# A decoder kernel: self and cross attention taken in turn batch by batch, cross with one product per head, gates on 128 rows

## The chip, the cores and the metric

The kernel runs on one core of one Trainium2 chip. The metric is the device time of one execution in microseconds (us). A core has TensorE for matrix products (PE; its weight loads are listed apart as PEld), VectorE (DVE), ScalarE (ACT), GpSimd (POOL) and the SyncE queue (SP), which here only starts DMA transfers. Each engine takes its own instructions strictly in the order in which the program gives them; engines wait for each other by semaphores. Products land in PSUM, eight banks of 128 rows by 512 values.

## The reference

32 sequences ("batches") of 128 positions and 128 channels go through two decoder layers. In layer 0, self attention, cross attention and a mixture of gated experts each read a layer-normalised copy of x and add to x. Layer 1 (causal attention, a latent cross attention, experts with ReLU) comes after and isn't touched.

```python
# layer 0, per batch of x (128, 128); 16 heads of 8 channels
h = layernorm(x)
q, k = rope(h @ Wq + bq), rope(h @ Wk + bk);  v = h @ Wv + bv
x = x + softmax(q k^T / sqrt(8)) v @ Wo + bo               # self attention
h = layernorm(x)
q = h @ Wq' + bq';  k, v = ctx @ Wk' + bk', ctx @ Wv' + bv'  # ctx (128, 96)
s = clip(q k^T / sqrt(8), -1e4, 1e4)
x = x + softmax(s) v @ Wo' + bo'                            # cross attention
h = layernorm(x);  g = top2_gates(h @ router)               # 8 routed experts, 2 shared
x = x + sum_e g[e] * (silu(h @ w1[e]) * (h @ w3[e])) @ w2[e]
```

If anything in the cross scores is not a number, the reference replaces the attention by a constant; the kernel keeps a copy of x (x_before) for that case.

## The kernel before

One call of `attention` handles self and cross attention: 32 self batches, then 32 cross batches, in 16 groups of 4. Each engine runs a list of steps. `ORDERS` gives, for a kind of attention and an engine, the steps of one slot n in order; `steps` (L293) walks n, turns each entry into a batch or group and sorts what falls into the slot by **place in its list divided by the length of that list**. A plain name works on batch n plus a fixed lead (`AHEAD`): T, f0, f1, e0, e1, x0, x1 on n itself; m (on PE and on ACT), mc, q0, q1 on n+1; s0, s1, m0, m1, km2 on n+2; km on n+3; w and n on n-1; y and a on n-2. An entry such as `k^6` works on a whole group, once, in the slot 6 ahead of the group's first batch.

The steps, by engine:

- PE: `s0 s1` scores by query into the two S banks (L407 ff.), each waiting until DVE has reduced the pair before; `T` scores by key into four T banks, 12 products, waits for POOL's masked queries and for the exponentials of the batch before; `m` turns the row maxima round (L463); `f0 f1` subtract the maxima from T (L450); `w` multiplies probabilities by values (L465 ff.); `y` the output projection; group steps `x c` transpose inputs, `k k2 q q2 v` project them (L387 to L389). y, x, c and all projections share one bank, PB, and each waits until the one before has been read.
- ACT: `m` copies the negated maxima (L560); `e0 e1` exponentials of two T banks each (L553); `ln` layernorm (L588); `xh ch kh qh` round to a high part; `k q` evict cross projections.
- DVE: `m0 m1` row maxima (L626); `x0 x1` clip cross scores in place in T (L632); `a` adds the output to x; `n` normalises the heads; `q q2 k k2` rotate self projections; `mo` moments; `xl cl cs ks qs v` low parts, sums and values.
- POOL: `mc` clips cross maxima (L807), waiting for m1; `km km2` masked keys and `q0 q1` masked queries (L784), one tile of 128x512 each; `kt qt` finish the rotation; `kl ql` low parts (L780); `rs` four small steps that turn moments into deviations (L752 to L758); `bo` adds the bias to x.

Moments, deviations and normalised input have one buffer each for all groups: `mo` of a group waits for `rs` of the group before it, `rs` for that group's `ln`. Tiles of keys and queries have two places, used in turn by group number.

Self attention multiplies each head's probabilities once, by values with a column of ones (`ONE_PASS`, 16 products, 32 records in the trace for one batch), and `n` has four DVE steps: transpose, reciprocal, product, transpose. Cross attention multiplies twice, by the values and by `head_ones` (L484, 32 products, 64 records), and `n` has two steps: a reciprocal of 128x128 and a product.

In the experts, `transpose_gates` turns 16 columns of gates into 16 rows, ACT copies them, and `spread_gate` multiplies them by a selection of 16 rows.

## Time and profile before

| | us |
|---|---|
| runs shown (3) | 1337.65, 1343.76, 1350.34 |
| their median | 1343.76 |
| the profiled execution | 1335.86 |
| its span, first to last instruction | 1333.8 |

| engine | busy us | share of the span |
|---|---|---|
| PE | 1108.2 | 83% |
| PEld | 825.9 | 62% |
| DVE | 887.8 | 67% |
| ACT | 675.6 | 51% |
| POOL | 792.0 | 59% |

Loading and set-up fill the first 45 us or so, self attention runs to about 270, cross attention to 512, the gated experts to about 700, and layer 1 from there. Shares over the whole span mix stages with different limits, so the stages are read one by one. A matmul's end is modelled in the profile, so a busy PE is not a PE at its peak. PEclk is the granted TensorE clock as a share of 2.4 GHz. In a view by stretches, the number after a stretch is its length, and each engine's busy time has its instructions in brackets. A row of the timeline merges equal instructions that follow each other; the bracket at its end is the idle time of the engine before it and what ended that.

### The profile page before, as it was taken

The page shows a single profiled execution, that of the slowest core. Times are in us where ns is not written, and L with a number is a line of the kernel's source. Part 1 is how long each engine was busy: PE and PEld are TensorE (multiplying, and loading weights), DVE is VectorE, ACT ScalarE, POOL GpSimd, SP SyncE. Part 2 cuts the span into 40 slices and gives each one's busy share as a digit, 9 for nine tenths or more (in the row PEclk, how much of TensorE's full clock was granted, in tenths as well). Part 3 has the DMA queues.
Part 4 walks back from the last instruction along what each step waited for, and adds up shares of the span by engine and source line. Part 5 has one row for each costly group of instructions (what it writes and reads, how often), then busy time and mean ns, then how long its engine had stood idle before and what let it go on. Part 6 is the DMA issues. An engine that isn't in the chain of part 4 may idle for free. (4 is left out here: it accounts for less than half of the span.)

```text
span 1333.8 us, 30226 instructions
## 1 busy us (share of the span) xinstructions
PE 1108.2 (83%) x10619; PEld 825.9 (62%) x10619; DVE 887.8 (67%) x2152; ACT 675.6 (51%) x1304; POOL 792.0 (59%) x895
## 2 busy tenths in 40 slices
PE   1799997788888886899969999993799886599992
PEld 0566665555555556566636766662788885488881
DVE  3588887579999994766536777764799886322223
ACT  1355554435545442455425565645888653255551
POOL 4788875546555552444446766743888676754542
PEclk9999998679999997799979999995999887699996
DMA  9930000000000000000000000000000002376665
GB/s 345 381 112 2 2 2 7 9 15 16 16 22 15 10 10 1 0 1 1 1 0 2 2 2 2 2 2 19 13 13 8 13 26 78 114 216 199 195 188 192
DMA packets 51556, 75.20 MB, mean 56 GB/s; under 512 B 13118, under 2 KB 31683, under 8 KB 51152
## 3 DMA queue, kind: packets, MB, share of 16 engines
q1 hardware_dynamic: 43344, 60.57, 14.4%
q0 software_dynamic: 4544, 8.47, 1.9%
q10 hardware_dynamic: 3520, 4.23, 0.9%
q8 instruction: 87, 1.43, 0.4%
q14 instruction: 61, 0.50, 0.1%
HBM read 40.37 MB, written 31.70 MB: 54 GB/s over the span
## 5 line engine op out<-in xcount | busy, mean ns | idle before, releaser
L626 DVE TENSOR_REDUCE maxes<-bank 128x8 f32<-128x1024 f32 x192 | 233.6, 1217 | 52.1 <-PE bank L418 51.2
L553 ACT ACTIVATE self_probs<-bank 128x1024 f32<-128x1024 f32 x128 | 129.0, 1022 | 45.2 <-PE bank L450 44.7
L1521 POOL DMA_INDIRECT returned<-relu_y,relu_slots x78 | 76.3, 979 | 68.4 <-DVE relu_y L1497 55.0
L1458 ACT ACTIVATE relu_hidden<-bank,cols 128x256 f32<-128x256 f32 x156 | 73.8, 473 | 77.1 <-PE bank L1417 77.1
L784 POOL TENSOR_TENSOR self_k_hi_m<-self_kq_hi,const 128x512 fp32r<-128x512 f32 x64 | 66.5, 1039 | 74.8 <-ACT self_kq_hi L581 74.8
L560 ACT ACTIVATE self_neg_max<-bank 128x512 fp32r<-128x512 f32 x64 | 38.2, 596 | 133.2 <-PE bank L463 133.2
L1417 PE MATMUL bank<-latent_kq,relu_w_tile 128*128 128x256 f32 x312 | 94.8, 387 | 0.5 <-DVE latent_kq L1491 0.5
L1425 PE MATMUL bank<-relu_hidden,relu_w_tile 128*128 128x256 f32 x312 | 93.1, 381 | 0.0
L1491 DVE COPY latent_kq<-bank 128x256 f32<-128x256 f32 x39 | 16.6, 425 | 100.2 <-PE bank L1407 100.2
L632 DVE TENSOR_SCALAR bank<-bank 128x1024 f32<-128x1024 f32 x64 | 78.2, 1224 | 3.3 <-PE bank L438 3.3
L2402 POOL DMA_INDIRECT routed<-latent_rows,latent_place_i x64 | 62.6, 979 | 24.4 <-issue 22.2
L450 PE MATMUL bank<-self_neg_max,const_r 32*128 32x512 f32 x256 | 62.8, 481 | 9.2 <-DVE bank L632 5.7
L1310 POOL TENSOR_TENSOR ffn_hidden<-ffn_product,ffn_gate 128x512 f32<-128x512 f32 x32 | 41.0, 1280 | 44.0 <-ACT ffn_gate L1068 36.1
L553 ACT ACTIVATE causal_probs<-bank 128x1024 f32<-128x1024 f32 x64 | 64.4, 1021 | 4.9 <-PE bank L450 2.5
L784 POOL TENSOR_TENSOR self_q_hi_m<-self_kq_hi,const 128x512 fp32r<-128x512 f32 x64 | 66.6, 1040 | 0.2 <-PE bank L450 0.2
L784 POOL TENSOR_TENSOR self_q_lo_m<-self_kq_lo,const 128x512 fp32r<-128x512 f32 x64 | 66.5, 1039 | 0.2 <-issue 0.2
L784 POOL TENSOR_TENSOR causal_q_lo_m<-causal_kq_lo,const 128x512 fp32r<-128x512 f32 x32 | 33.5, 1046 | 55.1 <-PE bank L450 55.0
L463 PE MATMUL bank<-ident,maxes 128*128 128x128 f32 x384 | 65.3, 295 | 0.5 <-POOL maxes L807 0.3
L1425 PEld LDWEIGHTS bank<-relu_hidden,relu_w_tile 128*128 128x128 f32 x312 | 59.8, 192 | 8.2 <-ACT relu_hidden L1458 0.2
L433 PE MATMUL bank<-self_q_hi_m,self_kq_hi 32*128 32x512 f32 x256 | 33.7, 503 | 36.3 <-ACT self_probs L553 35.1
L463 PEld LDWEIGHTS bank<-ident,maxes 128*128 128x128 f32 x384 | 42.9, 145 | 32.7 <-issue 24.1
L418 PE MATMUL bank<-self_k_hi_m,self_kq_hi 32*128 32x512 f32 x256 | 59.7, 455 | 4.0 <-DVE maxes L626 2.6
(402 smaller groups left out, 3432.8 us busy)
## 6 DMA issues: line engine op xcount, KB each, us to landing
relu_w_tile<-in_w_ffn SPq DMA_DIRECT2D x39, 512.0 KB, 3.7
routed<-blank SPq DMA_DIRECT2D x1, 19760.0 KB, 61.2
relu_slots<-routed SPq DMA_DIRECT2D x39, 130.0 KB, 3.1
x_all<-in_x SPq DMA_DIRECT2D x8, 256.0 KB, 8.3
x_before<-x_all SPq DMA_DIRECT2D x8, 256.0 KB, 2.3
relu_back<-returned SPq DMA_DIRECT2D x4, 512.0 KB, 8.0
latent_mask_rows<-returned ACTq DMA_DIRECT2D x4, 512.0 KB, 8.5
self_ctx_in<-in_ctx SPq DMA_DIRECT2D x8, 192.0 KB, 2.4
```

What stands on the lines that cost most here:

```text
L418: mm = pe.matmul(s_bank(u), kq_hi[QUERY][(n // GB) % 2][rows_of(u), batch_cols(n)], k_hi_m[n % 2][rows_of(u), :, :], start=not causal, sto ...
L450: mm = pe.matmul(t_bank(u), cr[rows_of(u), C_ONES + u * P:C_ONES + (u + 1) * P], neg_max[n % 2][rows_of(u), :], start=False, stop=True, sk ...
L463: mm = pe.transpose(OM[:, j * P:(j + 1) * P], maxes[n % 2][:, j * P:(j + 1) * P], sb["ident"][:, :])
L553: act.activation(probs[n % 2][:, 2 * pair:2 * pair + 2, :, :].rearrange("p u j q -> p (u j q)"), T[:, 2 * pair * GT:(2 * pair + 2) * GT], ...
L626: dve.tensor_reduce(out.rearrange("p j u -> p u j"), S.rearrange("p (u j k) -> p u j k", u=2, j=U), AX.X, ALU.max, negate=True).then_inc(m ...
L632: dve.tensor_scalar(t, t, CLAMP / scale, -CLAMP / scale, ALU.min, ALU.max).then_inc(clipped, 1)
L784: pool.tensor_tensor(out[n % 2][:, :, :], src[(n // GB) % 2][:, batch_cols(n)].bitcast(F32).unsqueeze(1).broadcast_to([P, U, P]), slots.un ...
L1417: pe.matmul(HT[i % 2][:, 0:TT], w_tile[t % NW][:, c * P:(c + 1) * P], s[t % 2][:, :], start=True, stop=True)\
L1425: pe.matmul(YT[t % 2][:, 0:TT], w_tile[t % NW][:, F1 + c * P:F1 + (c + 1) * P], hidden[i % C1][:, :], start=c == 0, stop=c == C1 - 1).then ...
L1458: act.activation(hidden[i % C1][:, :], HT[i % 2][:, 0:TT], ACT.Relu, bias=sb["cols"][:, bass.ds(r + (COL_RELU + c), 1)]).then_inc(hidden_d ...
L1521: pool.indirect_dma_start(returned[:, :], bass.IndirectOffsetOnAxis(ap=slots[t % NX][:, b, P:P + 1].bitcast(I32), axis=0), y[t % NY][:, b, ...
L2402: pool.indirect_dma_start(routed[:, :], bass.IndirectOffsetOnAxis(ap=place_i[u % 3][:, k, b:b + 1], axis=0), rows[G % 4][:, k, n % GB, :], ...
```

## The change

- Order of the batches: 14 self batches, then self 14, cross 0, self 15, cross 1 and so on for 18 pairs, then the last 14 cross batches. Cross batch b so stands right behind self batch 14 + b. Group steps keep their lists; cross leads grow by one (rs by two), and they count slots of both kinds. `-` is an empty place: it only moves the later places of DVE's self list.
- Keys and queries get four pairs of tiles, two for each kind, as do the values.
- Cross attention uses the one product per head and the four-step normalisation of self attention. Values lie in runs of 48 columns: two heads of the four share a run.
- The gates are written into 128 columns, zero beyond 16, so that the transposed gates, their copy and the selection have 128 rows. The tile is zeroed once.
- Set-up loses `head_ones`; SP's copies of x into x_before are written as a helper in the same order.

The core of the diff:

```diff
+HALF = 16
+ALONE = 14
...
     "self": {
         "PE": "T s0 f0 m y f1 q^5 s1 k^6 x^7 w k2^6 q2^5 v^4",
         "ACT": "ln^7 m e0 qh^3 xh^7 kh^5 e1",
-        "DVE": "m0 a q^5 mo^10 k^6 m1 xl^7 n v^4 k2^6 q2^5",
+        "DVE": "m0 - a - - q^5 mo^10 k^6 m1 xl^7 n v^4 k2^6 q2^5",
         "POOL": "qt^3 bo^6 rs^8 kl^2 km2 kt^4 q1 ql^2 q0",
     },
     "cross": {
-        "PE": "T s0 k^3 m y x^4 f0 w q^3 f1 s1 c^4 v^3",
-        "ACT": "m xh^4 kh^3 e0 q^3 qh^3 e1 ch^4 ln^5 k^4",
-        "DVE": "cs^3 cl^3 x0 mo^7 a x1 m0 xl^4 n m1 qs^1 ks^2 v^3",
-        "POOL": "kl^1 ql^1 mc q1 q0 km bo^2 rs^5",
+        "PE": "T s0 k^4 m y x^5 f0 w q^4 f1 s1 c^5 v^4",
+        "ACT": "m xh^5 kh^4 e0 q^4 qh^4 e1 ch^5 ln^6 k^5",
+        "DVE": "cs^4 cl^4 x0 mo^8 a x1 m0 xl^5 n m1 qs^2 ks^3 v^4",
+        "POOL": "kl^2 ql^2 mc q1 q0 km bo^3 rs^7",
...
+    batches = [(k, b) for k in kinds for b in range(B)]
+    if len(kinds) == 2:
+        batches = [(kinds[0], b) for b in range(ALONE)] + \
+            [batch for b in range(B - ALONE) for batch in ((kinds[0], ALONE + b), (kinds[1], b))] + \
+            [(kinds[1], b) for b in range(B - ALONE, B)]
+    groups = [(k, b // GB) for k, b in batches if b % GB == 0]
...
+    def before(G, steps):
+
+        k, g = groups[G]
+        return nth_group(k, g - steps) if g >= steps else None
+
+    def through(G):
+
+        k, g = groups[G]
+        return batches.index((k, GB * g + GB - 1)) + 1
+
+    def place_of(G):
+
+        k, g = groups[G]
+        return 2 * kinds.index(k) + g % 2
...
+                    if name == "-":
+                        continue
                     first = n + int(lead) if lead else n + AHEAD[name]
-                    if first // B == number and not (lead and first % GB):
-                        found.append((place / len(order), number, name, first // GB if lead else first))
+                    if not 0 <= first < NBT or kind(first) != k or lead and number_in_group(first):
+                        continue
+                    found.append((place / len(order), number, name, group(first) if lead else first))
...
+        kq_hi = [[buf(f"kq_hi{i}{j}", [P, GT], F32R) for j in range(2 * len(kinds))] for i in range(2)]
+        kq_lo = [[buf(f"kq_lo{i}{j}", [P, GT], F32R) for j in range(2 * len(kinds))] for i in range(2)]
...
                 pe.wait_ge(exp_done, 2 * n + 2)
-                heads_free(n)
+                if n > 0:
+                    pe.wait_ge(heads_read, n)
                 pe.wait_ge(neg_max_done, min(n + 3, NBT))
-                pe.wait_ge(pb_read, pb_uses["v", n // GB])
-                if one_pass(n):
-                    out = HEADS.rearrange("p (t a c) -> p t a c", a=2, c=32)
-                    for j in range(U):
-                        for u in range(U):
-                            mm = pe.matmul(out[rows_of(u), :, j // 2, :], V_SUMS[(n // GB) % 2][:, n % GB, U * u + j, :],
-                                           probs[n % 2][:, u, j, :].rearrange("p (t c) -> p t c", c=32),
-                                           start=j % 2 == 0, stop=j % 2 == 1)
-                    mm.then_inc(weighted, 1)
-                    return
-                for of, c in ((lambda u, j: V[(n // GB) % 2][:, n % GB, U * u + j, :], 0),
-                              (lambda u, j: head_ones[:, j, :], P)):
-                    for j in range(U):
-                        for u in range(U):
-                            mm = pe.matmul(OM[rows_of(u), c:c + P], of(u, j), probs[n % 2][:, u, j, :],
-                                           start=j == 0, stop=j == U - 1)
+                pe.wait_ge(pb_read, pb_uses["v", group(n)])
+                out, v = HEADS.rearrange("p (t a c) -> p t a c", a=2, c=32), V[place_of(group(n))]
+                for j in range(U):
+                    for u in range(U):
+                        c = HALF * (j % 2)
+                        mm = pe.matmul(out[rows_of(u), :, j // 2, :], v[:, number_in_group(n), u, j // 2, c:c + 2 * HALF],
+                                       probs[n % 2][:, u, j, :].rearrange("p (t c) -> p t c", c=32),
+                                       start=j % 2 == 0, stop=j % 2 == 1)
...
             def normalise(n):
...
-                dve.reciprocal(recip[n % 2][:, :], OM[:, P:2 * P]).then_inc(recip_done, 1)
+                if n > 0:
+                    dve.wait_ge(shares_done, n)
+                dve.transpose(by_query[:, :, :].rearrange("p h c -> p (h c)"), HEADS).then_inc(heads_read, 1)
+                dve.wait_ge(heads_read, n + 1)
+                dve.reciprocal(recip[:, :], by_query[:, :, DH]).then_inc(recip_done, 1)
                 dve.wait_ge(recip_done, n + 1)
+                if n > 0:
+                    dve.wait_ge(heads_done, n)
+                dve.tensor_tensor(shares[:, :, :], by_query[:, :, 0:DH], recip[:, :].unsqueeze(2).broadcast_to([P, H, DH]),
+                                  ALU.mult).then_inc(shares_done, 1)
+                dve.wait_ge(shares_done, n + 1)
                 if n - 1 > 0:
                     dve.wait_ge(out_projected, n - 1)
-                dve.tensor_tensor(o_t[n % 2][:, :], OM[:, 0:P], recip[n % 2][:, :], ALU.mult).then_inc(heads_done, 1)
+                dve.transpose(o_t[n % 2][:, :], shares[:, :, :].rearrange("p h d -> p (h d)")).then_inc(heads_done, 1)
...
                 for j in range(U):
                     at = lambda x: x.rearrange("p (u j d) -> p u j d", u=U, j=U)[:, :, j, :]
-                    tile, c = (V_SUMS, HALF * (j % 2)) if of_group(G) in ONE_PASS else (V, DH * j)
-                    op = dve.tensor_tensor(tile[G % 2][:, :, j:H:U, c:c + DH],
+                    c = 2 * HALF * (j % 2)
+                    op = dve.tensor_tensor(V[place_of(G)][:, :, :, j // 2, c:c + DH],
...
             def moments(G):
-                if of_group(G) == "self" and G >= 2:
+                k, g = groups[G]
+                if k == "self" and g >= 2:
                     dve.wait_ge(x_ready, 16 * (NG - 2))
-                if G >= NG:
-                    dve.wait_ge(pb_read, pb_uses["y", GB * (G - NG) + GB - 1])
+                if k == "cross":
+                    dve.wait_ge(pb_read, pb_uses["y", through(nth_group("self", g)) - 1])
                 if G > 0:
                     dve.wait_ge(mean_done, GB * G)
                     dve.wait_ge(rstd_done, G)
                 for b in range(GB):
-                    dve.bn_stats(stats[:, b, :], x_of(GB * G + b)).then_inc(stats_done, 1)
+                    dve.bn_stats(stats[:, b, :], x_group(G)[:, b * P:(b + 1) * P]).then_inc(stats_done, 1)
...
             def lo_of(G, i):
                 pool.wait_ge(hi_done, rounded[("kh", "qh")[i], G])
-                if G > 1:
-                    pool.wait_ge(shifted, 2 * (GB * G - GB))
-                    if of_group(G - 2) == "cross":
-                        pool.wait_ge(lo_summed, sums[("ks", "qs")[i], G - 2])
-                pool.tensor_tensor(kq_lo[i][G % 2][:, :], full[i][:, :], kq_hi[i][G % 2][:, :].bitcast(F32),
+                last = before(G, 2)
+                if last is not None:
+                    pool.wait_ge(shifted, 2 * through(last))
+                    if of_group(G) == "cross":
+                        pool.wait_ge(lo_summed, sums[("ks", "qs")[i], last])
+                place = place_of(G)
+                pool.tensor_tensor(kq_lo[i][place][:, :], full[i][:, :], kq_hi[i][place][:, :].bitcast(F32),
...
+                def keep(g):
+                    G = nth_group("cross", g)
+                    sp.wait_ge(biased, biases["bo", G])
+                    if g > 0:
+                        sp.wait_ge(x_kept, 16 * g)
+                    sp.dma_start(x_group(G, "x_before"), x_group(G)).then_inc(x_kept, 16)
+
                 for G in range(NG):
                     if G > 0:
                         sp.wait_ge(c_transposed, G)
@@ -840,13 +862,8 @@
                         .then_inc(ctx_loaded, 16)
 
                     if G > 0:
-                        sp.wait_ge(biased, G0 + G)
-                        if G > 1:
-                            sp.wait_ge(x_kept, 16 * (G - 1))
-                        sp.dma_start(x_group(G - 1, "x_before"), x_group(G - 1)).then_inc(x_kept, 16)
-                sp.wait_ge(biased, G0 + NG)
-                sp.wait_ge(x_kept, 16 * (NG - 1))
-                sp.dma_start(x_group(NG - 1, "x_before"), x_group(NG - 1)).then_inc(x_kept, 16)
+                        keep(G - 1)
+                keep(NG - 1)
...
-        gate_parts = buf("gate_parts", [P, GB, 2 * E0], F32R)
-        g_parts = [buf(f"g_parts{i}", [2 * E0, GT], F32R) for i in range(2)]
+        gate_parts = buf("gate_parts", [P, GB, P], F32R)
+        g_parts = [buf(f"g_parts{i}", [P, GT], F32R) for i in range(2)]
...
-                sel = cr[0:2 * E0, C_PAIR + k * P:C_PAIR + (k + 1) * P]
+                sel = cr[:, C_PAIR + k * P:C_PAIR + (k + 1) * P]
...
-                    mm = pe.transpose(LG[0:2 * E0, b * P:(b + 1) * P], gate_parts[:, b, :].bitcast(F32), sb["ident"][:, :])
+                    mm = pe.transpose(LG[:, b * P:(b + 1) * P], gate_parts[:, b, :].bitcast(F32), sb["ident"][:, :])
...
-                copy(g_parts[n % 2][:, :], LG[0:2 * E0, :], g_done)
+                copy(g_parts[n % 2][:, :], LG[:, :], g_done)
...
+                    if s == 18 and n == 0:
+                        dve.wait_ge(constants, 3)
...
+            pool.memset(gate_parts[:, :, :].bitcast(F32), 0.0).then_inc(constants, 1)
+            pool.wait_ge(constants, 3)
...
-                "v": [buf(f"values{i}", [P, GB, H, 32]) for i in range(2)],
-                "v_sums": [buf(f"values_sums{i}", [P, GB, H, 32]) for i in range(2)],
-                "head_ones": buf("head_ones", [P, U, 32]),
+                "v": [buf(f"values{i}", [P, GB, U, 2, 3 * HALF]) for i in range(4)],
...
```

## Rows read from the trace of the kernel before

**Rows 1.** Steady self, cross: length, busy PE, PEld, DVE, ACT, POOL; PEclk, DMA, GB/s
```profile
103.30:198.50 95.20, 89.02 (x1043) 59.79 (x1041) 83.09 (x173) 51.44 (x76) 78.77 (x81) 1.00 0.01 2
299.80:422.90 123.10, 102.42 (x1547) 71.52 (x1545) 116.39 (x181) 61.52 (x88) 72.81 (x93) 1.00 0.06 17
```
**Rows 2.** ACT's copies of row maxima (L560) by stretch: length, busy, count, PEclk
```profile
103.30:198.50 95.20, 9.56 (x16) 1.00 0.01 2
299.80:422.90 123.10, 9.52 (x16) 1.00 0.06 17
209.30:293.10 83.80, 5.37 (x9) 0.71 0.04 12
```

**Rows 3.** Timeline of slots of self attention with few group steps: start, us, what
```profile
209.90 1.94 ACT L553 ACTIVATE self_probs<-bank 128x1024 f32<-128x1024 f32 x2
213.33 0.66 PE L463 MATMUL bank<-ident,maxes 128*128 128x128 f32 x4
214.02 0.60 ACT L560 ACTIVATE self_neg_max<-bank 128x512 fp32r<-128x512 f32 x1 [2.19 <-PE bank L463]
214.49 0.50 PE L418 MATMUL bank<-self_k_hi_m,self_kq_hi 32*128 32x512 f32 x2
214.92 1.08 PE L475 MATMUL bank<-self_probs,values_sums 128*32 128x128 f32 x32
215.03 1.23 DVE L626 TENSOR_REDUCE maxes<-bank 128x8 f32<-128x1024 f32 x1 [0.40 <-PE bank L418]
```

**Rows 4.** Timeline in cross attention: maxima to clipped maxima to masks; T to clipping
```profile
358.86 1.22 DVE L626 TENSOR_REDUCE maxes<-bank 128x8 f32<-128x1024 f32 x1
...
360.28 0.22 POOL L807 TENSOR_SCALAR maxes<-maxes 128x16 f32<-128x16 f32 x1 [1.55 <-DVE maxes L626]
...
361.45 1.04 POOL L784 TENSOR_TENSOR self_q_hi_m<-self_kq_hi,const 128x512 fp32r<-128x512 f32 x1
...
376.82 0.51 PE L433 MATMUL bank<-self_q_hi_m,self_kq_hi 32*128 32x512 f32 x4 [0.17 <-ACT self_probs L553]
...
377.81 1.23 DVE L632 TENSOR_SCALAR bank<-bank 128x1024 f32<-128x1024 f32 x1 [0.24 <-PE bank L438]
```

**Rows 5.** DVE's timeline: first and last step of `n`, self, then cross
```profile
159.74 0.44 DVE L639 STREAM_TRANSPOSE self_by_query<-bank 128x256 f32<-128x256 f32 x1
...
160.91 0.31 DVE L650 STREAM_TRANSPOSE self_o_t<-self_shares 128x128 f32<-128x128 f32 x1
...
373.62 0.95 DVE L652 RECIPROCAL self_recip<-bank 128x128 f32<-128x128 f32 x1
374.60 0.29 DVE L656 TENSOR_TENSOR self_o_t<-bank,self_recip 128x128 f32<-128x128 f32 x1
```

**Rows 6.** Group steps: one line of the groups by line, then timeline rows
```profile
L780 POOL TENSOR_TENSOR self_kq_lo<-self_full,self_kq_hi 128x512 fp32r<-128x512 f32 x28 | 35.7, 1289 | 0.0
...
215.42 1.64 ACT L588 ACTIVATE self_xn<-x_all,self_shift_ln,self_rstd 128x128 f32<-128x128 f32 x4
...
235.62 0.87 DVE L689 BATCH_NORM_STATS2 self_stats<-x_all 128x6 f32<-128x128 f32 x4
236.64 0.38 DVE L693 BATCH_NORM_AGGREGATE self_mean_var<-self_stats 128x2 f32<-128x6 f32 x4
...
254.52 0.19 POOL L752 TENSOR_SCALAR self_var_eps<-self_mean_var 128x4 f32<-128x4 f32 x1
...
256.22 0.20 POOL L758 TENSOR_TENSOR self_shift_ln<-self_shift_ln,self_rstd 128x4 f32<-128x4 f32 x1
```

**Rows 7.** Weight loads of 128 columns in the gated experts, by line: busy, mean ns, idle
```profile
L984 PEld LDWEIGHTS bank<-ident,ffn_xn 128*128 128x128 f32 x32 | 3.9, 159 | 11.8 <-ACT ffn_xn L1089 10.3 <-issue 1.4
```

**Rows 8.** In the seam: PE's wait, the stretch after it, a product later
```profile
218.11 0.50 PE L433 MATMUL bank<-self_q_hi_m,self_kq_hi 32*128 32x512 f32 x4 [2.11 <-ACT self_probs L553]
...
220.40:223.80 3.40, 2.75 (x14) 1.35 (x14) 1.12 (x3) 1.38 (x3) 0.00 (x0) 0.50 0.00 0
...
238.04 1.94 PE L475 MATMUL bank<-self_probs,values_sums 128*32 128x128 f32 x32
```

More of the change, by code:

```diff
@@ L241, in attention, with group, number_in_group, nth_group @@
     KEY, QUERY = 0, 1
+    batches = [(k, b) for k in kinds for b in range(B)]
[4 more added lines that the diff above has]
+    groups = [(k, b // GB) for k, b in batches if b % GB == 0]
     def kind(n):
-        return kinds[n // B]
+        return batches[n][0]
     def of_group(G):
-        return kinds[G // NG]
+        return groups[G][0]
+    def group(n):
+        k, b = batches[n]
+        return groups.index((k, b // GB))
+    def number_in_group(n):
+        return batches[n][1] % GB
+    def nth_group(k, g):
+        return groups.index((k, g))
+    def before(G, steps):
[7 more added lines that the diff above has]
+        return 2 * kinds.index(k) + g % 2
     def weight(G, name, rows=P):
@@ L264, in attention @@
     slots = sb["const"][:, U:2 * U]
-    V, V_SUMS, maxes, head_ones = sb["v"], sb["v_sums"], sb["maxes"], sb["head_ones"]
-    def one_pass(n):
-        return kind(n) in ONE_PASS
+    V, maxes = sb["v"], sb["maxes"]
     def x_of(n):
-        return sb["x"][:, n % B * P:(n % B + 1) * P]
+        b = batches[n][1]
+        return sb["x"][:, b * P:(b + 1) * P]
     def x_group(G, tile="x"):
-        return sb[tile][:, G % NG * GT:(G % NG + 1) * GT]
+        g = groups[G][1]
+        return sb[tile][:, g * GT:(g + 1) * GT]
     S, T = bank[:, 0:2 * GT], bank[:, 2 * GT:6 * GT]
@@ L319, in attention @@
     rounded, remainders = count("ACT", ("kh", "qh")), count("POOL", ("kl", "ql"))
+    biases = count("POOL", ("bo",))
     turns, sums = count("POOL", ("kt", "qt")), count("DVE", ("ks", "qs"))
@@ L377, in batch_cols, with number @@
         def batch_cols(n):
[L378 removed]
+            i = number_in_group(n)
+            return slice(i * P, (i + 1) * P)
+        def number(n):
+            return batches[n][1]
         def parts_of(G):
@@ L574, in hi_of @@
             def hi_of(G, i):
-                if G > 1:
-                    act.wait_ge(shifted, 2 * (GB * G - GB))
+                if before(G, 2) is not None:
+                    act.wait_ge(shifted, 2 * through(before(G, 2)))
                 if of_group(G) == "self":
```

105 lines of the change are left out of this document (36 added, 69 removed).

## The prediction

> **What bounds the kernel now.** I read the attention phase first by stretches, because only it and one detail of the next phase change. In a steady stretch of self attention, the first line of [rows 1], DVE is busy 83.09 of 95.20 us, PE 89.02, POOL 78.77; in steady cross attention, its second line, DVE is busy 116.39 of 123.10 (95%), PE 102.42, POOL 72.81. The copy of the row maxima (L560) runs once a batch, so counting it gives the rate [rows 2]: 16 batches in 95.2 us are 5.95 us per self batch, 16 in 123.1 us are 7.69 per cross batch. Cross is bound by DVE; self is bound by nobody alone, but by the loop from scores to exponentials to the next scores, well packed with DVE work. The third stretch is the seam, 9 batches in 83.8 us where 5 self and 4 cross batches at their own rates would take 5 x 5.95 + 4 x 7.69 = 60.5. So the seam loses 23.3 us, and TensorE's clock there is 0.71. That is the only visible prize.
>
> **The slots after the change.** A slot is one pass of the sorted step lists. In the mixed part even slots belong to a self batch (S), odd ones to a cross batch (C); a step that looks 1 ahead or behind is of the other kind. Sorting by place over list length gives, without the group steps:
> DVE in C: x0 a x1 m0 m1 n; in S: m0 a m1 n. PE in C: T s0 m y f0 f1 w s1; in S: T s0 f0 m y f1 s1 w. ACT in both: m e0 e1. POOL in S: mc q1 **km2** q0 km; in C: q1 q0.
> The point is km2, the masked keys that s0 of the same S slot needs. Before, in self alone, km2 stood ahead of q1 and there was no mc. Now it stands behind mc, which waits for m1 of the C slot before, the last reduction DVE makes there. PE then sits at s0, and behind it are queued f0, m, y, f1, and through them ACT's exponentials and the next T.
>
> **A bare pair (C then S, no group step).** Times count from the end of x1 in C. Pieces: a reduction occupies DVE 1.2 us, and one follows 0.54 after its scores start (214.49 to 215.03); w takes 1.08; the maxima's transposes 0.66, their copy 0.60 (0.5 until the next ACT step), two exponentials 1.94 [rows 3]. After m1 ends (358.86 + 1.22) mc starts 0.20 later, and the second mask 1.17 after mc's start, so a mask costs 1.0 in a row of them; clipping takes 1.2 and starts 1.0 after T [rows 4]. The four-step n takes 1.5 (159.74 to 161.22), against 1.27 for cross's own two steps (373.62 to 374.89) [rows 5].
> C: m0 0 to 1.2; f1, then w, then s1 at 1.4; m1 1.95 to 3.15; n to 4.6. POOL: mc 3.35, q1 3.5, km2 4.55 to 5.6. S: s0 5.7, f0 5.95, m0 6.25 to 7.45, transposes 6.25 to 6.9, copy 6.95, e0 and e1 7.45 to 9.4, next T 9.5, ready for x0 at 10.5. DVE: a, m1 8.05 to 9.25 (s1 at 7.5), n to 10.65. Then x0, a, x1 end at **13.3**. DVE stands idle about 1.6 at m0 and 0.8 at C's m1.
> A pair at the old rates, its share of group steps included, is 5.95 + 7.69 = 13.64. So almost all room for group steps is gone before any is placed.
>
> **The group steps, in a cycle of 8 slots** (self groups begin in slots 2 modulo 8, cross groups in 7). Prices: kl or ql 1.28 on POOL, the four rs steps 1.9 (254.52 to 256.42), layernorm on ACT 1.65, moments 1.25 on DVE (235.62 to 236.9) [rows 6]; projections on PE about 1, evictions 0.6 to 0.7 and the remaining DVE steps 0.7 to 0.85 are estimates from the 512-column masks, copies and transposes in [rows 3, 4].
> - Slots 6, 7: v after n (0.85) and moments between x0 and x1 (1.25) land on DVE's own path: +2.1.
> - Slots 0, 1: kl stands between mc and q1. Worse, self's moments in slot 0 need the single statistics buffer that cross's rs releases, and that rs is last in POOL's slot: 3.35 + 0.25 + kl 1.28 + four masks 4.1 + ql 1.28 + rs 1.9 = 12.1. Moments end at 13.4 where m1 should have begun at 8.05: +5.35. Behind it wait m1, n and x0.
> - Slots 2, 3: self's rs stands ahead of mc and waits for cross's layernorm on ACT (1.64 + 1.65 + 1.9 = 5.2, mc +1.85). On ACT the rounding of x stands ahead of e0 and that of the context ahead of e1, each behind a transposition that waits for the one projection bank: e1 ends at 14.3 instead of 9.4. The context's two DVE steps come next; x0 starts at 15.75 instead of 10.65 (+5.1). Then a waits for y behind the key projection and its eviction (+1.45): +6.55.
> - Slots 3 to 5: f1 of slot 3 stands behind q's eviction and x's transposes, and ACT has run layernorm first, so m1 comes 2.75 late; in slot 4 the k rotation on DVE waits for a projection that is now behind s1 and w (+2.6); two DVE steps after n (+1.35); in slot 5 the q rotation waits for its projection ahead of x1 (+1.75): +8.45.
> Four pairs: 4 x 13.3 + 2.1 + 5.35 + 6.55 + 8.45 = 75.65, against 4 x 13.64 = 54.56. That is 9.46 us per slot. The only stretch of before in which both lists share slots, the seam, gives 83.8 / 9 = 9.3 [rows 2]; I take the walk.
>
> **The sum.** Mixed part, 18 pairs: 4.5 x (75.65 - 54.56) = +95. Seam gone: -23.3. The longer n in the 14 cross batches that stay alone and are bound by DVE: 14 x (1.5 - 1.27) = +3; in the mixed part it is in the walk. The second product for the sums, another 1.08 of PE per cross batch, goes, but DVE covers it; without that cover it would give back 15 on those 14 batches. Gates over 128 rows: 32 weight loads grow from 16 to 128 columns; bounds are 0 and the whole of such loads, 32 x 0.159 = 5 [rows 7]; I take 1, as the moving side keeps its columns. Zeroing the gate tile costs POOL at most one mask (1.04) while it waits for the first moments: 0. The memsets at the start only shrink: 0. SP's queue keeps its order, a context load then a copy of x, both asked for slots before use: 0. Sum +76. The profiled execution took 1335.9, so **1412**. The median of the three runs stands 7.9 above that execution, within their spread; I leave it to the range.
>
> **Rivals.**
> *DVE stays the bound (faster).* If waits in one slot are filled by group steps of the other kind, a pair costs its old 13.64 and only the seam counts: 1335.9 - 23.3 + 3 = 1316. For it: POOL has 50 us idle in the cross stretch and DVE's total hardly grows [rows 1]. Against it: km2's place behind mc is a matter of order, not of load. It decides once the mixed slots average under (18 x 13.64 + 23.3 - 4) / 36 = 7.3 us. Chance 0.16.
> *The group steps hide.* The bare pair holds, but the steps fill its holes and only those after n, before x0 or before x1 count, 7.1 per four pairs (k2 and ks 1.35, v 0.85, cs and cl 1.25, q 0.75, moments 1.25, and about 1.6 of moments, x and k before m1): 15.1 per pair, 18 x 1.45 = +26, total 1335.9 + 26 - 23.3 + 4 = 1343. For it: PE and POOL idle half of such a pair. Against: moments need rs, not a hole. Chance 0.12.
> *The clock falls too.* In the seam PE waits 2.11 us at T for ACT, and in the next stretch the granted clock is 0.50, the lower level of 1.2 GHz; there w takes 1.94 instead of 1.08 [rows 3, 8]. In the mixed part PE waits 2.9 us at s0 in every bare pair, longer in others. At the lower level w gives +0.86, the transposes about +0.5, and each of the two T's, scores and shifts about +0.85 by the same ratio: +3.1 per pair, +56 over 18, 1468 in all. Chance 0.22.
> The Trainium skill (TensorE: Matmul & The Clock Gate, section "Why this matters for your kernels") says that pauses between bursts of matmuls throw the array back to half clock; by it the clock rival would be the rule and not the exception, and the sum 1468. The seam agrees in part: 0.71 on average, not 0.50.
>
> **How the numbers follow.** The forecast, 1375 to 1440, has 0.50. The range must leave out no more than 0.2: it leaves out the first rival and a little above the third, 1338 to 1470; mine alone is 1375 to 1440. About 1% is what a measurement here can tell from no change. Faster is the first rival, 0.16; the second is half within 1% and half a little above, so same 0.08; slower 0.76.
>
> **What would show it.** Right: in the mixed part the maxima copies come about 9.4 us apart on average, DVE is busy under 75%, and PE's s0 in the S slots waits for POOL's key mask, about 3 us after mc; DVE waits in one slot of eight for rs. The lone parts keep 5.95 and 7.7 to 7.9. Wrong: mixed slots near 7 us, or POOL reaching km2 before m1 ends; then the order of the queues does not bind and the seam's 23 us come off. A clock near 0.5 with the same order of waits would mean that only the size is off.

## The result and the profile after

The changed kernel takes 1495.66 us (median of 4 runs, 1492.11 to 1500.8), the kernel before beside it 1345.24: a ratio of 1.117, 95% interval 1.112 to 1.122. Forecast were 1412 and a range up to 1470. The direction was right; the loss is twice the forecast.

The page of the changed kernel, its span and its busy times:

```profile
span 1490.3 us, 28293 instructions
## 1 busy us (share of the span) xinstructions
PE 1213.6 (81%) x9595; PEld 888.2 (60%) x9595; DVE 906.6 (61%) x2216; ACT 676.3 (45%) x1304; POOL 790.3 (53%) x891
```

PE has 1024 records of products fewer than before (a cross batch loses 16 small products, two records each) and is busy 105 us longer; DVE has 19 us more, ACT and POOL are within 2 us. The stretches tell why. Windows of the changed kernel, cut at the copies of the row maxima (now L578): batches 0 to 9, 9 to 14, 14 to 50 (the mixed part) and 50 to 63; columns as in [rows 1]:

```profile
52.16:103.45 51.29, 47.35 (x512) 30.94 (x511) 43.29 (x88) 26.85 (x41) 42.49 (x45) 1.00 0.50 180
103.45:157.25 53.80, 43.94 (x340) 29.51 (x340) 26.94 (x59) 19.79 (x31) 25.51 (x26) 0.62 0.03 9
157.25:549.00 391.75, 305.44 (x2320) 196.10 (x2318) 235.57 (x436) 126.39 (x182) 166.61 (x192) 0.62 0.02 6
549.00:657.61 108.61, 92.37 (x806) 58.74 (x805) 91.17 (x145) 44.40 (x59) 52.71 (x66) 0.69 0.03 10
```

The same batch numbers before, from the times of L560, beside the terms of the forecast (profiled executions, 1335.86 and 1492.11):

| batch numbers | before | after | difference | forecast |
|---|---|---|---|---|
| 0 to 9, self alone | 51.13 | 51.29 | 0 | 0 |
| 9 to 14, self, first group steps of cross among it | 29.46 | 53.80 | +24 | 0 |
| 14 to 50 (before: with the seam) | 268.26 | 391.75 | +123 | +95 - 23 |
| 50 to 63, cross alone | 96.45 | 108.61 | +12 | +3 |
| all the rest | | | -4 | +1 |

From the second stretch on the mean granted clock is 0.62 to 0.69, nearer the lower level (0.50) than the full one, where [rows 1] had 1.00 in both kinds.

The waits that were forecast are there. From the timeline of a steady cycle (start, length, what; in brackets the idle time before it and what ended it):

```profile
274.04 1.23 DVE L644 TENSOR_REDUCE maxes<-bank 128x8 f32<-128x1024 f32 x1 [2.18 <-PE bank L442]
275.47 0.22 POOL L822 TENSOR_SCALAR maxes<-maxes 128x16 f32<-128x16 f32 x1 [10.15 <-DVE maxes L644]
...
277.90 1.04 POOL L799 TENSOR_TENSOR self_k_hi_m<-self_kq_hi,const 128x512 fp32r<-128x512 f32 x1
...
278.99 0.79 PE L442 MATMUL bank<-self_k_hi_m,self_kq_hi 32*128 32x512 f32 x2 [4.05 <-POOL self_k_hi_m L799]
...
284.29 0.87 DVE L701 BATCH_NORM_STATS2 self_stats<-x_all 128x6 f32<-128x128 f32 x4 [2.27 <-POOL self_shift_ln L771]
...
294.31 0.20 POOL L765 TENSOR_SCALAR self_var_eps<-self_mean_var 128x4 f32<-128x4 f32 x1 [8.16 <-ACT self_xn L606]
...
296.30 0.22 POOL L822 TENSOR_SCALAR maxes<-maxes 128x16 f32<-128x16 f32 x1
```

POOL stands 10.15 us at mc (L822) until DVE has made the last maxima; km2 (277.90) comes third behind it, after kl and q1, and PE's s0 (L442) starts when km2 ends. The moments wait for rs (L771), and self's rs (L765) waits for cross's layernorm with mc behind it. And the clock: it first falls in the entry, where T waits 2.25 us (to 114.43) for an exponential queued behind layernorm on ACT. Windows ahead of that wait and behind it:

```profile
105.00:113.50 8.50, 7.03 (x104) 5.02 (x104) 7.75 (x24) 4.56 (x9) 3.00 (x4) 1.00 0.01 2
114.40:117.40 3.00, 1.66 (x12) 0.90 (x12) 0.00 (x0) 0.00 (x0) 2.92 (x4) 0.50 0.00 0
```

### The profile page after: what moved, and what is told of

Its sections match the earlier page's. It is cut to its first block and busy times, and to the rows that moved or that the text cites. A ratio compares the mean times of both kernels' runs of the same rounds, so it can differ in the third digit from the quotient of the medians.

```text
span 1490.3 us, 28293 instructions
## 1 busy us (share of the span) xinstructions
PE 1213.6 (81%) x9595; PEld 888.2 (60%) x9595; DVE 906.6 (61%) x2216; ACT 676.3 (45%) x1304; POOL 790.3 (53%) x891
## 3 DMA queue, kind: packets, MB, share of 16 engines
q1 hardware_dynamic: 43344, 60.57, 12.5%
## 5 line engine op out<-in xcount | busy, mean ns | idle before, releaser
L578 ACT ACTIVATE self_neg_max<-bank 128x512 fp32r<-128x512 f32 x64 | 38.1, 595 | 246.8 <-PE bank L488 246.8
L822 POOL TENSOR_SCALAR maxes<-maxes 128x16 f32<-128x16 f32 x32 | 7.0, 217 | 216.6 <-DVE maxes L644 216.4
L442 PE MATMUL bank<-self_k_hi_m,self_kq_hi 32*128 32x512 f32 x256 | 78.6, 606 | 47.8 <-POOL self_k_hi_m L799 37.7
L501 PE MATMUL bank<-self_probs,values 128*32 128x128 f32 x2048 | 107.8, 378 | 3.2 <-ACT self_neg_max L578 2.5
L474 PE MATMUL bank<-self_neg_max,const_r 32*128 32x512 f32 x256 | 82.1, 635 | 21.7 <-DVE bank L650 21.7
L501 PEld LDWEIGHTS bank<-self_probs,values 128*32 128x32 f32 x2048 | 78.7, 151 | 34.1 <-issue 25.7
L488 PE MATMUL bank<-ident,maxes 128*128 128x128 f32 x384 | 82.4, 352 | 0.0
L442 PEld LDWEIGHTS bank<-self_k_hi_m,self_kq_hi 32*128 32x128 f32 x256 | 33.7, 254 | 80.2 <-POOL self_k_hi_m L799 48.0
L488 PEld LDWEIGHTS bank<-ident,maxes 128*128 128x128 f32 x384 | 54.2, 175 | 42.5 <-issue 36.5
L457 PE MATMUL bank<-self_q_hi_m,self_kq_hi 32*128 32x512 f32 x256 | 46.2, 639 | 26.7 <-ACT self_probs L571 26.5
```

Of the source, the lines that this page charges most:

```text
L442: mm = pe.matmul(s_bank(u), kq_hi[QUERY][place_of(group(n))][rows_of(u), batch_cols(n)], k_hi_m[n % 2][rows_of(u), :, :], start=not causal ...
L474: mm = pe.matmul(t_bank(u), cr[rows_of(u), C_ONES + u * P:C_ONES + (u + 1) * P], neg_max[n % 2][rows_of(u), :], start=False, stop=True, sk ...
L488: mm = pe.transpose(OM[:, j * P:(j + 1) * P], maxes[n % 2][:, j * P:(j + 1) * P], sb["ident"][:, :])
L501: mm = pe.matmul(out[rows_of(u), :, j // 2, :], v[:, number_in_group(n), u, j // 2, c:c + 2 * HALF], probs[n % 2][:, u, j, :].rearrange("p ...
```

## The experiments

The theory on trial: alternating costs time by the order of the queues (as forecast), and on top of it by the clock, which falls because PE waits. The rivals stand in each expectation. A time without a ratio is that of one profiled execution; the kernel before ranged from 1332 to 1352 us, so single times tell 20 us apart and not 5. Batches 0 to 9 (51 to 65 us) and what comes behind attention (828 to 846 us) differ from one profile shown here to the next too, so a total follows the mixed part only roughly. The stretches "mixed part" and "lone cross" are always batch numbers 14 to 50 and 50 to 63.

### Is it the alternation?

```diff
-ALONE = 14
+ALONE = 32
```

> ALONE = 32: all self batches, then all cross batches; one product per head, four pairs of tiles, the leads and the gates stay as changed. Theory (alternating costs it all): mixed part and entry vanish (-146 - 24), the seam of before comes back (+23), so about 1345 + 3 to 8 for the longer normalisation, 1347 to 1355. Rival (one product leaves TensorE too idle in cross, and its clock falls there, as in the lone cross batches of the changed kernel, 8.35 instead of 7.42 us a batch): 32 x 0.93 = +30, about 1375, with a granted clock near 0.7 in cross. Second rival (the cost lies in the layout or the tiles, not in alternating): above 1450.

1372.66 us, 1.022 times the kernel before (1.016 to 1.028). So alternating costs 123 of the 150 us, and the first rival is right about the rest: without any alternation 27 to 29 us remain, and the clock in cross is 0.71 (26 batches, 8.60 us each; before 7.60).

```diff
-ALONE = 14
+ALONE = 26
```

> The changed kernel with ALONE = 26: six mixed pairs instead of 18, 26 lone cross batches. Theory (the loss is per pair, and the entry into the mixed part costs what the old seam cost): between the not alternated kernel (0 pairs, 1372.7) and the changed one (18 pairs, 1495.7) on a line, 1372.7 + 6 x 6.8 = 1414. Rival (entering and leaving the mixed part costs 24 us and more by itself, however few pairs): 1372.7 + 24 + 6 x 5.5 = 1430 or more. Second rival (it takes many pairs until the clock has fallen): under 1400.

1413.41: on the line. The loss is 6.8 us per pair. The entry, here batches 21 to 26, is the same as in the changed kernel (53.80 us at 0.62):

```profile
174.62:228.71 54.09, 44.01 (x340) 29.37 (x340) 26.95 (x59) 19.79 (x31) 25.51 (x26) 0.62 0.03 9
```

Without alternation these five batches take 29.5, so the entry costs some 24 us, as the old seam cost 23.3; the loss has moved, not gone.

### One product, and the clock

In the kernel before, alone:

```diff
-ONE_PASS = ("self", "causal")
+ONE_PASS = ("self", "cross", "causal")
```

> The kernel before with one edit: cross attention takes the one product per head and the four-step normalisation of self. No alternation, old tiles, old leads, old gates. Theory (the second product kept TensorE busy enough for its full clock; without it the clock of the cross stretch stays at its lower level and DVE waits for the output projection): granted clock about 0.7 instead of 1.00 in the cross stretch, 8.4 to 8.6 us a batch instead of 7.7, +20 to +30 us, 1360 to 1370. Rival (the loss of the not alternated kernel comes from its leads and tiles; the one product costs only the longer normalisation): +3 to +5, 1343 to 1346, clock 1.00. Second rival, the step as predicted blind: nothing but the normalisation, which is the same number.

1370.16, ratio 1.024 (1.018 to 1.031): the product that was taken away costs 26 us. Then the same, with that product computed twice:

```diff
-                    for j in range(U):
+                    for j in 2 * list(range(U)) if kind(n) == "cross" else range(U):
                         for u in range(U):
```

> The kernel before with one product per head in cross (the edit that alone cost 26 us), and this product computed twice: TensorE has the 64 records a batch of before again, at the same place, and the four-step normalisation stays. Theory (the loss is the clock, which fell because TensorE had less to do): clock 1.00 again from 300 us on, 7.7 to 7.9 us a cross batch, 1345 to 1352. Rival (the normalisation's length or the place of its steps loses it): 1365 to 1375, as with one product.

1348.89, ratio 1.007 (1.004 to 1.011). The window from 300 to 490 us with one product:

```profile
300.00:490.00 190.00, 165.83 (x1385) 107.69 (x1389) 159.61 (x282) 84.98 (x123) 96.72 (x122) 0.70 0.04 13
```

and with it twice:

```profile
300.00:490.00 190.00, 158.86 (x2249) 110.73 (x2241) 170.13 (x302) 90.51 (x130) 103.11 (x132) 0.94 0.05 14
```

With 864 more records of products PE is busy 7 us less, as its clock is 0.94 and not 0.70, and DVE, which bounded this stretch before [rows 1], works 10.5 us more in the same time. What DVE waits for longest there (total us, times, longest), with one product:

```profile
DVE x_all L718 <- PE bank L497: 12.0, 15, 2.2
```

and with it twice:

```profile
DVE self_by_query L639 <- PE bank L475: 9.2, 9, 2.7
DVE x_all L718 <- PE bank L497: 2.3, 3, 1.2
```

At the low clock the output projection comes late to DVE's `a`; with the copies that wait goes, and a smaller one, for the doubled product itself, comes. A cross batch takes 7.60 us before, 8.71 with one product, 7.99 with it twice. So of the 26 us about 17 are the clock; 9 stay with the longer normalisation, a clock not quite at 1.00, and that later product, which aren't separated.

It is not a long wait that lowers the clock here. The same window of the kernel before, at 1.00, and PE's longest wait in it:

```profile
300.00:490.00 190.00, 157.76 (x2401) 110.14 (x2400) 178.50 (x270) 93.30 (x131) 109.75 (x138) 1.00 0.05 15
...
PE bank L433 <- ACT self_probs L553: 16.2, 25, 1.0
```

and with one product, at 0.70:

```profile
PE bank L433 <- ACT self_probs L553: 8.7, 19, 0.9
PE bank L418 <- DVE maxes L626: 7.3, 11, 1.3
```

PE stands idle 32 us of the 190 before and 24 with one product. That the number of products decides the clock here is shown, by taking them away and putting them back; by what rule is not.

The same edit in the not alternated and in the changed kernel:

> ALONE = 32, and cross does its one product twice (the same 64 records a batch as before, the same place). Theory (clock): the granted clock of the lone cross stretch returns to 0.9 to 1.00 and most of the 30 us that the not alternated kernel lost there come back, although TensorE works more: 1345 to 1358. Rival (the loss there is the longer normalisation and the leads): no return, 1372 or up to 15 more.

1364.31 (ratio 1.015, 1.010 to 1.020) against 1372.66, between what theory and rival asked for: the intervals overlap, so this pair alone decides nothing.

> The changed kernel, but cross repeats its product of probabilities and values (32 more small products a batch with the same result), so that TensorE is as busy there as with the two products of before. Theory (the lone cross batches are slow by the clock that fell with the second product): in them the granted clock goes from 0.69 to 1.00 and 13 batches (#50 to #63) from 108.6 to 97 to 100 us; the mixed part changes by -20 to +35, total 1465 to 1520. Rival (the longer normalisation on DVE makes them slow): 108.6 stays or grows, and the clock's level doesn't matter.

1510.78. The lone cross batches have 0.90 instead of 0.69 and take 106.36 instead of 108.61: the expected gain of 9 did not come. Against the clock theory's size, but the copies stand between the exponentials and DVE's `n` here too. The mixed part is 399.45 at 0.69, +8.

### Order, in the mixed part

```diff
-        "POOL": "qt^3 bo^6 rs^8 kl^2 km2 kt^4 q1 ql^2 q0",
+        "POOL": "km2 qt^3 bo^6 rs^8 kl^2 kt^4 q1 ql^2 q0",
```

> The changed kernel with km2 as the first step of POOL's self list, so that the masked keys no longer stand behind mc. Theory (the place of km2 behind mc is what each pair pays first): the waits of s0 for the masked keys (8 slots: 17.9 us of it) go; what DVE does next is n, so 1.65 us a pair come back at full clock and up to 3.5 at the lower one, 18 pairs: 1430 to 1466. Rival (several queues end together, the next wait takes its place): under 15 us, above 1480.

1470.14; the mixed part is 361.08, that is 30.7 less, 1.7 a pair. The edit also moves self's rs behind mc, since all places shift. PE's longest waits in the mixed part of the changed kernel:

```profile
PE bank L442 <- POOL self_k_hi_m L799: 36.0, 14, 4.0
PE bank L474 <- DVE bank L650: 18.0, 19, 2.0
PE bank L457 <- ACT self_probs L571: 14.2, 6, 6.8
```

and of this one:

```profile
PE bank L474 <- DVE bank L650: 18.1, 18, 2.0
PE bank L442 <- DVE maxes L644: 14.2, 13, 4.2
PE bank L457 <- ACT self_probs L571: 12.8, 6, 5.8
```

36.0 us at the masked keys are gone; 14.2 at the maxima (3.0 in the changed kernel) take part of their place. How much of the 30.7 is km2 and how much rs isn't separated.

```diff
-        "POOL": "kl^2 ql^2 mc q1 q0 km bo^3 rs^7",
+        "POOL": "rs^7 kl^2 ql^2 mc q1 q0 km bo^3",
```

> The changed kernel with rs as the first step of POOL's cross list instead of its last. Theory (self's moments wait in one slot of eight until POOL has done kl, four masks, ql and then cross's rs): 5.35 us predicted for each of the 4.5 cycles, -15 to -25 us, 1470 to 1480, and the wait of DVE's moments for POOL's shift goes. Rival (the moments' wait is taken over by the wait for the masked keys, as rs now stands ahead of the masks): -5 to +10.

1475.91, mixed part 363.91 (-27.8), and the wait of the moments for POOL (6.8 us in three waits in the changed kernel) is no longer among DVE's longest. The gain is four times that wait; the clock is 0.66 instead of 0.62, and what the rest comes from isn't shown.

```diff
-        "ACT": "ln^7 m e0 qh^3 xh^7 kh^5 e1",
+        "ACT": "ln^7 m e0 qh^3 xh^7 kh^5 e1 - -",
```

with both edits above:

> The changed kernel with three edits of order: km2 first in POOL's self list, rs first in its cross list (each alone gave 31 and 28 us in the mixed part), and ACT's self list lengthened by two empty places, so that e1 of self stands ahead of the rounding of the context and of the layernorm of cross. Theory (the mixed part is set by the order of the queues, and these are separate terms): the mixed part from 392 to about 392 - 31 - 28 - 4.5 x 3 = 320, with 5 more from the entry; total 1415 to 1435. Rival (the terms overlap, since each repair exposes the next wait): mixed part 345 to 360, total 1450 to 1465.

1466.60, mixed part 354.57 at 0.70. The rival holds for the mixed part: 31 + 28 alone, 37 together with ACT's edit. PE stands idle there for 86.3 us in the changed kernel, 67.4 with km2 first alone and 74.8 with all three: other waits take the place of the repaired ones. The longest left are f behind the clipping (21.4 us, 18.0 in the changed kernel) and T behind the exponentials (17.3, 14.2).

### PE kept busy, order unchanged

```diff
...
                 if step == "T":
+                    if len(kinds) == 2 and i >= ALONE and kind(i) == "self":
+                        for _ in range(4):
+                            key_scores(i, alone=True)
                     key_scores(i)
...
```

A copy (`alone=True`) writes the same banks and signals nothing.

> The changed kernel, but in every S slot of the mixed part TensorE computes the key scores T four times more before the real ones (the same values into the same banks, no new wait), which fills part of its wait at s0. Theory (the fall of the clock makes about 50 us of the loss): the granted clock of the mixed part rises from 0.62 towards 1.00 and the time falls although TensorE has 18 x 2.8 = 50 us more to do at full clock: 1440 to 1470. Rival (the clock is low because the engine waits, and costs nothing of itself): the clock may rise, the time doesn't fall: 1495 to 1545.

1486.38. Window of the mixed part:

```profile
158.12:531.41 373.29, 304.86 (x3184) 213.75 (x3182) 230.61 (x436) 126.74 (x181) 164.18 (x190) 0.80 0.02 7
```

18.5 us less than 391.75, with 864 products more and the same order of steps, while the entry is unchanged (53.91 against 53.80): the clock costs time of itself. The total fell by 9 only (forecast 1440 to 1470), which one execution doesn't tell from nothing: the copies take time too, the clock reaches 0.80 and not 1.00, and the lone cross part lost 5.

> The kernel with the three edits of order, and three more copies of the key scores T in every S slot of the mixed part, as in the run that kept TensorE busy. Theory (clock beside order): the granted clock of the mixed part rises from about 0.66 to 0.8 or more, and it is 10 to 20 us shorter than with the three orders alone. Rival (with the wait at s0 repaired, the copies stand in the way): 0 to +40.

1464.67, and the mixed part is 363.63 at 0.77 against 354.57 at 0.70: the rival. Where the wait at s0 is repaired, the copies stand in the way; the total comes out even by the lone cross part (106.11 against 111.57) and by what follows attention (836 against 846).

What a low clock costs shows without copies where one slot of the cycle meets both levels. The stretches between the copies of batches 21 and 22, and of 37 and 38 (two cycles later, the same steps), in the changed kernel:

```profile
240.01:246.52 6.51, 5.63 (x62) 3.27 (x61) 3.70 (x8) 2.43 (x3) 5.16 (x5) 0.98 0.11 40
417.53:428.08 10.55, 9.71 (x64) 5.96 (x63) 5.72 (x10) 2.43 (x4) 5.33 (x5) 0.50 0.07 26
```

The stretches 23 to 24 and 31 to 32 in the kernel with km2 first:

```profile
252.00:260.74 8.74, 8.74 (x68) 6.65 (x68) 5.10 (x13) 2.41 (x5) 3.59 (x4) 0.50 0.00 0
335.60:340.78 5.18, 4.81 (x65) 3.74 (x66) 4.45 (x11) 2.40 (x5) 3.59 (x4) 1.00 0.02 3
```

At 0.50 PE is busy for 9.71 of 10.55 and 8.74 of 8.74 us and is the bound; near 1.00 the slot is 4.0 and 3.6 us shorter. In the first pair PE's products come in the same order in both stretches, and its only wait is the same 0.84 us.

### The same at the seam of the kernel before

The first edit lengthens ACT's self list of the kernel before by three empty places, so that e1 goes ahead of the rounding of the context and of cross's layernorm; the second adds one at the head of DVE's self list; the third computes T of batch 29 twice more. `steps` also learns to pass over `-`.

```diff
-        "ACT": "ln^7 m e0 qh^3 xh^7 kh^5 e1",
-        "DVE": "m0 a q^5 mo^10 k^6 m1 xl^7 n v^4 k2^6 q2^5",
+        "ACT": "ln^7 m e0 qh^3 xh^7 kh^5 e1 - - -",
+        "DVE": "- m0 a q^5 mo^10 k^6 m1 xl^7 n v^4 k2^6 q2^5",
...
                 if step == "T":
+                    if len(kinds) == 2 and i in (29,):
+                        for _ in range(2):
+                            key_scores(i, alone=True)
                     key_scores(i)
```

> The kernel before with one edit: three empty places at the end of ACT's self list, so that at the seam e1 of the last self batches stands ahead of the context's rounding and of cross's layernorm on ACT. In the seam T waits 4.26 and 1.69 us for that e1. Theory (these waits are what part of the 23 us of the seam hangs on): -4 to -10, 1334 to 1340. Rival (cross's group steps come later by as much, and the seam is limited by them): -1 to +5.

1332.09, ratio 0.994 (0.991 to 0.997), as the theory had it. The seam of the kernel before, batches 27 to 36:

```profile
209.40:293.17 83.77, 66.11 (x638) 44.35 (x636) 52.44 (x99) 32.86 (x48) 39.07 (x47) 0.71 0.04 12
```

With this edit it takes 77.10 (next fence): PE is busy as long as before (66.17), so waits were won and the clock was not.

> The kernel before with ACT's self list lengthened by three empty places (which alone gave 0.6%) and one empty place at the head of DVE's self list, so that at the seam the two context steps go ahead of the row maxima. With the first edit alone the granted clock of the seam falls to 0.50 at the place where TensorE waits 2.28 us for the context's low part, and stays there for 28 us in which TensorE hardly waits. Theory (that one wait costs the clock, and the clock costs the seam): the wait shrinks to about 1, the clock stays at 1.00 longer, the seam (nine batches, 77.1 us) comes to 66 to 72, total 1322 to 1330. Rival (the wait moves to the scores behind the row maxima, and the clock falls there): within 3 us of the first edit alone, 1330 to 1336.

1329.34, ratio 0.991 (0.988 to 0.995). The window of the seam (batches 27 to 36) with the first edit alone, and in it the stretch behind the wait of 2.28 us:

```profile
215.86:292.96 77.10, 66.17 (x638) 44.58 (x636) 52.26 (x99) 33.00 (x47) 39.10 (x47) 0.71 0.04 13
...
234.00:262.00 28.00, 26.24 (x191) 17.57 (x190) 14.16 (x34) 11.45 (x17) 15.03 (x19) 0.53 0.03 11
```

The seam with both:

```profile
211.38:279.25 67.87, 55.36 (x638) 37.80 (x636) 51.54 (x99) 32.66 (x48) 39.12 (x47) 0.87 0.05 15
```

and there PE's longest single wait, at T for POOL's masked queries, and its wait for the context, in two parts:

```profile
PE bank L435 <- POOL self_q_hi_m L786: 2.2, 1, 2.2
...
PE bank L389 <- DVE self_c_lo L707: 1.2, 2, 0.6
```

Same products, same DVE work; the longest wait at that place falls from 2.28 to 0.6, the clock rises from 0.71 to 0.87, PE is busy 10.8 us less and the seam is 9.2 shorter. PE's idle time doesn't fall (10.9 us, then 12.5), so the gain is the clock's. The rival is right that a wait moves: at T PE now waits 2.2 us, and the next 6.60 us (236.00 to 242.60) are at 0.50; but by 242.70 the clock is at 1.00 again. The seam of before took 83.77, so 15.9 of its 23.3 us of loss [rows 2] are won without any alternation. The totals of the two versions can't be told apart (0.994 and 0.991, intervals overlapping); each is faster than both kernels.

> The kernel with both edits at the seam, and the key scores of one batch (29) computed twice more, 1.4 us of TensorE at full clock where it would wait for the context. Theory (clock): what is left of that wait is filled, the clock of the seam stays at 1.00, another 0 to -6. Rival (the copies only delay the scores): +1 to +3.

1326.09, ratio 0.991 (0.988 to 0.995); the seam is 69.10 at 0.85, not 1.00. The intervals cover each other: the copies gave nothing more that can be measured. The wait they were meant to fill was nearly gone.

### The gates alone

> The kernel before with one edit: the gates over 128 rows. Predicted blind: +1 (0 to +5), from wider weight loads. What the profiles of both versions say now: the 32 products that spread the gates take 0.409 us each instead of 0.512, and the stage of the experts has one stretch at the lower clock less; theory: -3 to -5. Rival: the shorter products are covered by POOL's and ScalarE's steps behind them: 0 to +1.

1344.47, ratio 1.002 (0.998 to 1.006): nothing that can be measured. The edit is the whole part of the diff inside the experts, put into the kernel before. Its products with the selection, by line, before and with this edit:

```profile
L964 PE MATMUL bank<-ffn_g_parts,const_r 16*128 16x512 f32 x32 | 16.4, 512 | 1.4 <-ACT ffn_gate L1068 0.7 <-ACT ffn_g_parts L1068 0.7
...
L964 PE MATMUL bank<-ffn_g_parts,const_r 128*128 128x512 f32 x32 | 13.1, 408 | 1.4 <-ACT ffn_gate L1068 0.7 <-ACT ffn_g_parts L1068 0.7
```

They take 408 ns each, 512 before, 3.3 us in all; the loads of the gates, now 128 columns, take 145 ns instead of 93. The rival fits better than the theory (-3 to -5, which lies just outside the interval): something else covers the shorter products, and what it is wasn't tested.

## Why the prediction was right in direction and wrong in size

The step that failed is the price of the mixed part: the walk put every piece at full clock and the fall of the clock at nothing in the sum. The stretch came out 123 us longer and not 72, at a clock of 0.62. Two terms failed beside it: the seam's -23.3, which came back as +24 in the entry, and the second product's "DVE covers it", put at nothing, where the lone cross batches lost 9 us more than the +3 of the sum. With -5 for all the rest these make the 80 us between +76 and the +156 of the profiled executions.

**What bounds the kernel.** Read rightly from [rows 1, 2], with one gap: the clock of 1.00 there was taken as given, not as something that cross attention's second product kept up.

**The bare pair.** Right in its mechanism. km2 behind mc was put at a wait of 2.9 us per pair at s0; 14 recorded waits average 2.6. Moving it ahead, with rs moved too, gave 1.7 a pair.

**The group steps.** The two waits of rs are where the walk had them, as the timeline above shows. The surcharge of slots 0 and 1, 4.5 x 5.35 = 24, is near the 27.8 us that moving rs gave, but that is partly luck: the recorded waits of the moments are 2.3 us and not 5.35, three of them, 6.8 us in all. And such terms are not a sum: three repairs together gave 37 in the mixed part, not 59 and more.

**The mixed part, +95.** Too small by 51. The forecast kept the clock at its full level and made the fall a rival of 0.22, priced at +56 (1468), beside a forecast of 0.50 without it. The walk without the fall is a case that no run here shows: the order makes PE wait 2 us and more, and behind such waits the clock falls. Both terms belonged in one sum, 1335.9 + 95 + 56 = 1487, with nothing taken off for the seam. That it lies so near 1492 is partly luck, as the terms of the clock and of the waits can't be told apart. That the clock costs time by itself is shown (PE kept busy, the pairs of stretches, the seam); how many of the 51 us are its share isn't separated, since no run held the mixed part at 1.00. The Trainium skill (TensorE: Matmul & The Clock Gate, section "HAM oscillation — how this bites in real kernels") describes this pattern, waits between bursts (there for DMA) that put the array back to half clock; the trace agrees in the entry, with 0.50 right behind a wait of 2.25 us, and over the mixed part, with 0.62. The kernel before with one product goes further: its cross stretch had 0.70 with no wait over 1.3 us. The prediction named the same title and still gave the rule a chance below that of the walk; it read the seam's 0.71 as agreement in part. That 0.71 was a mean over stretches at 0.50 (220.40 to 223.80, [rows 8]) and at 1.00 (226.90 to 230.10 in the same trace).

**The seam gone, -23.3.** Wrong. More than half of the seam's loss (13.4 of 23.3 us) falls on batches 27 to 32, the last of self, where the first group steps of cross stand among self slots; they take 43.1 us and not 5 x 5.95. These steps now stand in the entry: +24 where nothing was put. The run with six pairs shows that entry and seam cancel.

**The longer normalisation, +3, and the shorter w, "DVE covers it".** Wrong in kind. The cover was taken for a question of DVE's time; the bound was right for that, but the removed product also kept up TensorE's clock. Alone its removal costs 26 us, some 17 of them by the clock. The text named 15 as what w would give back without cover; the sign was wrong.

**The gates, +1, the memsets and SP, 0.** No difference of the gates can be measured, so +1 can't be told from 0. Its parts were not all seen: the 32 loads grew by 1.1 us in all, as priced, but the products, expected to keep their time with their columns, became 3.3 us shorter. No engine's longest waits in the mixed part name a DMA, which agrees with SP at 0. The stages behind attention are 4 us shorter in one execution, within the spread.

**The signs to look for.** Copies 9.4 us apart: 10.9. DVE under 75% busy: 60% in the mixed part. s0 waiting for the masked keys, DVE for rs: both, the second in three recorded waits. A lone self part at its old rate: yes; lone cross at 7.7 to 7.9: no, 8.4. "A clock near 0.5 with the same order of waits would mean that only the size is off": that is what came, at 0.62, but for the entry and the lone cross part, where a term was missing.

## What to carry to other kernels

Before work is taken from TensorE, ask whether the rest keeps its clock up: at a lower clock a shorter stream of products can take longer, here 8.71 instead of 7.60 us a batch, 2.4% of the kernel. When in-order lists of two kinds are merged, walk one pair of slots through every queue, then take the granted clock of the nearest stretch with such waits, stretch by stretch and not as a mean, into the same sum. Before a border between two stages is dissolved, find the wait that makes it dear: here four empty places in two lists of the old kernel won 0.9%.

## What the hardware showed that was not expected

Taking 16 small products a batch away (32 records) lowered the mean granted clock of the cross stretch from 1.00 to 0.70, though PE's waits there grew neither in sum nor much in length, and computing one product twice brought it to 0.94. PE at 0.50 was busy 8.74 of 8.74 us in a slot that took 5.18 us at 1.00, so at the low clock TensorE itself was the bound of that slot. A wait of 2.28 us, the longest by far around it, stood at the beginning of 28 us at 0.53 in the seam; with two edits of order one of 2.2 us stood ahead of 6.60 us at 0.50. The selection of 128 rows ran in 408 ns where that of 16 rows took 512.
